# Three attentions over 4096 keys: three float32r products in place of one float32 product, in a loop over pairs of tiles

## The reference

```python
ctx_1024                     # (2, 4096, 256), keys and values alike
q = _layernorm(x) @ Wq + bq  # (2, 256, 256)
k = ctx @ Wk + bk
v = ctx @ Wv + bv
s = q @ k.T * scale          # (2, 256, 4096); layer 0 with a mask on keys
x = x + softmax(s) @ v       # layer 0: then @ Wo + bo
```

## Time and the profile before

| | us |
|---|---|
| median of 3 runs | 1531.21 (1530.9 to 1531.96) |
| profiled execution, its span | 1523.9 |
| what lies around the span, against the median | 7.3 |
| TensorE busy | 1475.2 (97%) |
| VectorE busy | 839.1 (55%) |
| ScalarE busy | 649.0 (43%) |
| GpSimd busy | 151.5 (10%) |

### The profile page before, as it was taken

The page is one execution under the profiler, slowest core; times in us unless marked ns, Lnnn a source line. Parts: engine busy times, 40 slices in busy tenths (PEclk is TensorE's granted clock), DMA queues, the critical chain, the costliest instruction groups (busy, mean ns, idle before and its releaser), DMA issues.

```text
span 1523.9 us, 24409 instructions
## 1 busy us (share of the span) xinstructions
PE 1475.2 (97%) x9937; PEld 945.5 (62%) x9937; DVE 839.1 (55%) x1502; ACT 649.0 (43%) x1231; POOL 151.5 (10%) x191
## 2 busy tenths in 40 slices
PE   8999999999999999999999999999999999999998
PEld 3668666887567755567755545555555554555697
DVE  4652645453433353333254268889999992566533
ACT  1312342212333233434263246777777777325232
POOL 0000330002100040400102050110000000100000
PEclk9999999999999999999999999999999999999999
DMA  9134132221012520103212456654675611410140
GB/s 375 64 111 172 62 110 90 89 94 50 25 55 77 209 81 8 60 28 116 97 29 106 146 126 143 95 82 67 125 166 112 125 23 72 190 56 1 53 169 14
DMA packets 42997, 147.61 MB, mean 97 GB/s; under 512 B 6380, under 2 KB 21996, under 8 KB 34028
## 3 DMA queue, kind: packets, MB, share of 16 engines
q1 hardware_dynamic: 42888, 146.07, 33.5%
HBM read 123.49 MB, written 22.56 MB: 96 GB/s over the span
## 4 chain that ended last, share of the span: by engine, by line
PE 87%; DVE 8%; ACT 3%; issue 1%; DMA 0%; SPq 0%; ACTq 0%; DVEq 0%
PE PS L162 55%; PE PS L2190 8%; PE PS L2102 7%; PE PS L2087 5%; PE PS L612 3%; PE PS L1451 2%; DVE SM L2206 2%; PE PS L1680 1%; PE PS L1701 1%; PE PS L2181 1%; PE PS L2776 1%; PE PS L1708 1%; PE PS L2681 1%; DVE SM L297 0%; DVE AR L895 0%
## 5 line engine op out<-in xcount | busy, mean ns | idle before, releaser
L2206 DVE TENSOR_REDUCE SM<-PS 128x1 f32<-128x1024 f32 x256 | 301.7, 1219 | 34.2 <-PE PS L2087 33.0
L162 PE MATMUL PS<-CT,HT 128*128 128x512 f32 x416 | 190.4, 593 | 0.7 <-ACT HT L719 0.7
L162 PE MATMUL PS<-CN,AR 128*128 128x256 f32 (+1 forms) x832 | 188.0, 371 | 0.0
L162 PEld LDWEIGHTS PS<-CN,AR 128*128 128x128 f32 x832 | 151.0, 190 | 44.0 <-issue 28.7
L2102 PE MATMUL PS<-AR 49*128 49x256 bf16 (+1 forms) x1216 | 162.8, 271 | 3.3 <-issue 2.0
L162 PE MATMUL PS<-HT,AR 128*128 128x512 f32 x328 | 150.3, 605 | 2.6 <-ACT HT L346 1.6
L2102 PE MATMUL PS<-AR,CT 49*128 49x256 bf16 (+1 forms) x832 | 124.3, 271 | 0.0
L669 DVE TENSOR_REDUCE SM<-AR 128x1 f32<-128x512 f32 x96 | 65.7, 686 | 97.2 <-ACT AR L725 95.6
L162 PEld LDWEIGHTS PS<-CT,HT 128*128 128x128 f32 x416 | 73.6, 190 | 68.4 <-issue 66.0
L162 PE MATMUL PS<-AR 128*128 128x256 f32 (+3 forms) x504 | 109.8, 372 | 1.4 <-DVE AR L647 0.8
L162 PEld LDWEIGHTS PS<-HT,AR 128*128 128x128 f32 x328 | 60.4, 192 | 76.0 <-issue 72.5
(11 more groups left out here) (373 smaller groups left out, 2118.9 us busy)
## 6 DMA issues: line engine op xcount, KB each, us to landing
CN<-ctx_n SPq DMA_DIRECT2D x24, 1024.0 KB, 4.7
AR<-k_parts SPq DMA_DIRECT2D x114, 128.0 KB
k_parts<-CN SPq DMA_DIRECT2D x32, 384.0 KB, 3.3
CT<-pack SPq DMA_DIRECT2D x6, 2048.0 KB, 8.3
AR<-pack SPq DMA_DIRECT2D x20, 512.0 KB, 4.6
CT<-k_parts SPq DMA_DIRECT2D x78, 128.0 KB
CT<-ctx_t SPq DMA_DIRECT2D x8, 1024.0 KB, 18.7
v_ones<-CN SPq DMA_DIRECT2D x28, 288.0 KB, 3.3
```

What stands on the lines that cost most here:

```text
L162: last = te.matmul(o, l, r, start=first and k == 0, stop=final and k == n - 1, skip_group_check=True)
L2206: ve.tensor_reduce(MX9[:, p % 2, e, g % 8 // 4, g % 4:g % 4 + 1], PS[:, b:b + 2, :].rearrange("p a b -> p (a b)"), AX, ALU.max).then_inc(* ...
```

## The change

`xattn` is rewritten; the rest of the program stays, but for places in AR, three waits of weight loads and the order of two things on GpSimd.

- Each operand of scores and mixes is held as a head, a copy of type float32r, and a rest, the difference between the float32 value and the head. A product becomes three: head x head, head x rest, rest x head.
- The loop runs over 16 steps g. A step is one tile and 1024 keys: `tile_of(g)`, `part_of(g)`; steps g and g + 1 (a pair of tiles) use the same two chunks of context, so a chunk k (16 in all) is split once for two tiles.
- Softmax runs over parts: VectorE takes the maximum of 1024 keys from PSUM (masked: from P), ScalarE makes the exponentials with the running maximum, and `add_mixed` rescales OB by `al`, the exponential of the change of the maximum, and adds the part.
- ScalarE makes the heads: `split_t(k)` of transposed context (128 x 1024), `split_n(k)` of context rows (128 x 1024), `head_of_weights` (128 x 512, twice a step).
- VectorE makes the rest of the weights, twice a step, and of the transposed context for k = 0 and 1; GpSimd makes it for k > 1, and the rest of the context rows for all k, in place over CN.
- Rings: context heads and rests of the transposed context 3 deep, heads of rows 3, turned weights 3, P 2, score banks 2 pairs, two banks for transposes (four from step 14), two for mixes.
- The loads of the next stages' weights wait for ("s_ps", s, 15, 1) instead of ("pt_ps", s, 2, 7); in stage 0 the mask's work tiles lie in CN, and `values_ones` runs behind the stage's GpSimd part.

In the diff below, the three loops over g are TensorE's, VectorE's and ScalarE's, in this order.

```diff
+                def score(g, h):
+                    k, t = chunk_of(g, h), tok(tile_of(g))
+                    if h == 0:
+                        _, before = SC.take(("s", s, g), ("s", s, g, 1) if masked else ("e", s, g))
+                        pe.wait_ge(*before, ("qnr", s, 0), ("qnr", s, 1))
+                    pe.wait_ge(("ctr", s, k))
+                    ch, cr = CTH[k % 3], CTR[k % 3]
+                    mm(te, PS[:, banks.of("s", s, g)[0] + h, :],
+                       [p for kt in range(2) for p in ((QNH[:, kt, t], ch[:, kt, :]), (QNH[:, kt, t], cr[:, kt, :]),
+                                                       (QNR[:, kt, t], ch[:, kt, :]))]).then_inc(
+                        *pe.inc("score", "s_ps", s, g, h))
...
+                def mix(g, h):
...
+                    pe.wait_ge(("ptr", s, g, h), ("cnr", s, k))
+                    ph, pr, nh, nr = PTH[u % 3], PTR[u % 3], CNH[k % 3], context_n(k, CNr)
+                    mm(te, bank("mix", s, g)[:, 0:256],
+                       [p for y in range(4) for p in ((ph[:, tok(y)], nh[:, y, :]), (ph[:, tok(y)], nr[:, y, :]),
+                                                      (pr[:, tok(y)], nh[:, y, :]))], h == 0, h == 1).then_inc(
+                        *pe.inc("mixed", "mix", s, g, h))
+                for g in range(2):
+                    score(g, 0)
+                    score(g, 1)
+                for g in range(14):
+                    turn(g, 0)
+                    score(g + 2, 0)
+                    turn(g, 1)
+                    mix(g, 0)
+                    score(g + 2, 1)
+                    mix(g, 1)
...
+            def rest_of_context(pr, k):
+                pr.wait_ge(("cth", s, k))
+                pr.e.tensor_tensor(CTR[k % 3], context_t(k), CTHf[k % 3], ALU.subtract).then_inc(
+                    *pr.inc("rest", "ctr", s, k))
...
+                for g in range(16):
+                    if g:
+                        add_mixed(g - 1)
+                    sums(g)
+                    rest_of_weights(g, 0)
+                    if masked and g + 2 < 16:
+                        masked_scores(g + 2, 0)
+                    rest_of_weights(g, 1)
...
+                    if g + 2 < 16:
                         if masked:
+                            masked_scores(g + 2, 1)
+                        largest(g + 2)
...
+                for g in range(16):
+                    head_of_weights(g, 0)
+                    if g + 1 < 16:
+                        exp(g + 1)
+                    head_of_weights(g, 1)
+                    if g + 4 < 16:
+                        split_t(g + 4)
+                    if g + 2 < 16:
+                        split_n(g + 2)
...
                 if s:
                     jobs_pool(pl, f"b{s}", *ht_all(s))
+                split_t(2)
+                split_n(0)
+                split_t(3)
+                split_n(1)
+                if s:
                     jobs_pool(pl, f"t{s}")
                 add_row_pool(pl, s, W["bo" if project else "bv"], *h_all(s), w, ("nb", s, 0))
+                for k in range(2, 16):
+                    if k + 2 < 16:
+                        split_t(k + 2)
+                    split_n(k)
...
-            sp.wait_ge(("pt_ps", 3, 2, 7))
+            sp.wait_ge(("s_ps", 3, 15, 1))
...
         def gpsimd_program(pl):
+            xattn_0[3](pl)
+            pl.wait_ge(("s", 0, 15, 1))
             values_ones(pl, (0, 1))
-            xattn_0[3](pl)
```

More of the change, by code:

```diff
@@ L14 @@
 I32 = mybir.dt.int32
+F32R = mybir.dt.float32r
 AX = mybir.AxisListType.X
@@ L599, in pe_part @@
                     half_pe(pe, f"h{s}", 1)
[L600 to L618, removed]
@@ L650, in dve_part @@
                 ve.tensor_copy(cadd, bank("c", s)[:, 0:4]).then_inc(*dv.inc("proj", "cadd", s))
-                for what, i, c in xattn_steps():
-                    if what == "chunk":
-                        o = S[i % 2][:, c * 512:c * 512 + 512]
-                        if masked:
[L655 to L688, removed]
@@ new lines, in dve_part, with bound @@
+                if not masked:
+                    rest_of_context(dv, 1)
+                for m in range(2):
+                    dv.wait_ge(("qnh", s, m))
+                    ve.tensor_tensor(QNR[:, m, :], bank("q2", s, m), QNHf[:, m, :], ALU.subtract).then_inc(
+                        *dv.inc("proj", "qnr", s, m))
+                if masked:
+                    rest_of_context(dv, 0)
+                    rest_of_context(dv, 1)
+                def bound(g, h):
+                    k = chunk_of(g, h)
+                    c = slice(k % 8 * 512, k % 8 * 512 + 512)
+                    dv.wait_ge(("mu", g // 8), ("s", s, *last_use(k - 8)) if k > 7 else None)
+                    ve.tensor_scalar(MB[:, c], MU[g // 8][:, c], 2 * BIG, -BIG, ALU.mult, ALU.add).then_inc(
+                        *dv.inc("bound", "bound", k))
@@ new lines, in masked_scores @@
+                def masked_scores(g, h):
+                    k = chunk_of(g, h)
+                    if g % 2 == 0:
+                        bound(g, h)
+                    dv.wait_ge(("s_ps", s, g, h), ("cadd", s), ("bound", k), ("pt_ps", s, g - 2, h) if g > 1 else None)
+                    ve.scalar_tensor_tensor(out=P[g % 2][:, h * 512:h * 512 + 512], in0=PS[:, banks.of("s", s, g)[0] + h, :],
+                                            scalar=of(cadd, tile_of(g)), in1=MB[:, k % 8 * 512:k % 8 * 512 + 512],
+                                            op0=ALU.add, op1=ALU.min).then_inc(*dv.inc("score", "s", s, g, h))
@@ new lines, in rest_of_weights @@
+                def rest_of_weights(g, h):
+                    u = 2 * g + h
+                    dv.wait_ge(("pth", s, g, h))
+                    ve.tensor_tensor(PTR[u % 3], bank("pt", s, g, h), PTHf[u % 3], ALU.subtract).then_inc(
+                        *dv.inc("turn", "ptr", s, g, h))
+                for g in range(2):
+                    if masked:
+                        masked_scores(g, 0)
+                        masked_scores(g, 1)
+                    largest(g)
+                if not ctr_by_pool(3):
+                    rest_of_context(dv, 3)
@@ L689, in dve_part @@
+                add_mixed(15)
                 if s == 0:
```

233 lines of the change are left out of this document (166 added, 67 removed).

## The result

The changed kernel takes 1560.32 us (median of 4 runs, 1556.19 to 1561.81) where the kernel before takes 1531.06 (1530.31 to 1531.96). The ratio is 1.0183, interval 1.0163 to 1.0202: **slower, by 29 us**. The forecast was 1491, its range ended at 1521. The prediction was wrong in sign, and the time lies outside its range.

What follows compares the result with a forecast made beforehand. TensorE was taken to bound the three loops; savings of 7.6, 17.0 and 15.2 us, together 39.8, cut the profiled span from 1523.9 to 1484.1, and 7.3 from span to median gave 1491 us, range 1462 to 1521.

Steps and rivals of the forecast that it cites:

- VectorE's chain: From a step's second score group to the next: 6.2 us, masked 6.98; with tile closings, steps of 6.31 and 7.09.
- three dependent small instructions at 0.18 to 0.20, 0.55: VectorE's small instructions after the reduction over 1024 scores, costed at 0.55 us of each step's chain.
- in the loops nearly all of VectorE's read PSUM: Reason given for expecting little contention between GpSimd and VectorE instructions with two SBUF inputs.
- GpSimd's late start: GpSimd's queue delays its first remainders, so TensorE waits early in each loop: 0.9, 4.35 and 6.2 us (loops 0, 3, 6).
- GpSimd paces it: Rival: GpSimd's remainders cost more, 3.08 or 3.5 us each, giving 1497 or 1519 us; chance 0.15.
- TensorE paced the kernel before: TensorE, busy nearly throughout the three loops, paces these 375 us; time falls only if it has less to do.
- One stream a float32r product, weight loads hidden: TensorE products at 0.216 us (scores) and 0.111 (mixes), making its step 6.15 us against 7.77.
- ScalarE's and GpSimd's durations: Work per step: ScalarE 4.9 us, heads of context 1.14 each; GpSimd 4.7, two remainders of 2.35; both beside TensorE's 6.15.
- Costed at nothing: Later loads of W1, W4, W7, SP's queue, values_ones and query heads add no time; uncovered, each load up to 13 us.
- two streams: Rival: a float32r product streams twice on TensorE, a step takes 11.2 us, the kernel 1705; chance 0.07.
- weight loads don't hide: Rival: each float32r load holds TensorE its whole 0.19 us, a step takes 8.04, the kernel 1559; chance 0.05.
- TensorE paces all: Rival: handoffs cheaper than counted, masked steps 6.15 instead of 7.09, no GpSimd stalls, 1462 us; chance 0.08.

Runs made afterwards that it cites:

- orders of 7: (5) with VectorE's first remainder of weights ahead of add_mixed and sums, and GpSimd's t job and additions to X later; also called experiment 7; 1490.28 us, ratio 0.9747.
- experiment 9: Changed kernel with only the two orders of 7 (remainder of weights first, GpSimd's t job and additions later), its own VectorE instructions kept; 1536.26 us, ratio 1.0041.
- experiment 1: Changed kernel with the second input of VectorE's small one-element instructions given as a pointer scalar instead of a second SBUF tensor; 1517.18 us, ratio 0.9921.
- (5): experiment 1 with the masks' bounds moved from VectorE to ScalarE; 1513.66 us, ratio 0.9879.
- experiment 6: experiment 1 with one instruction, nb (the negative of the largest), put back as a tensor_tensor of two SBUF columns; 1533.9 us, ratio 1.003.
- experiment 2: Changed kernel with each of GpSimd's context remainders as four instructions of 256 columns instead of one of 1024; 1550.78 us, ratio 1.0131.
- experiment 4: Changed kernel with only the head by head product in scores and mixes, the rests still made; single run, 1530.89 us.

## Why the prediction was wrong

The experiments make a table (us, number of the experiment; the kernel before was at 1529.5 to 1531.0 beside each):

```
                                 orders as changed    orders of 7
small ones with two SBUF inputs  1560.3               1536.3 (9)
pointer scalars                  1517.2 (1)
pointer scalars, bounds ScalarE  1513.7 (5)           1490.3 (7)
```

The pointer scalars are worth 43 us with the first orders and 1536.3 − 1490.3 − 3.5 = 42.5 with the others; the orders 24.0 and 23.4. The two causes add up, as far as a measurement tells; the 3.5 for the bounds is taken from the left column, and pointer scalars with the new orders and the bounds on VectorE were not run.

**The step that failed** is the term of VectorE's chain "three dependent small instructions at 0.18 to 0.20, 0.55", and with it the sentence that dismissed contention since "in the loops nearly all of VectorE's read PSUM". Nearly all of VectorE's *time* reads PSUM; of its *instructions* four or five a step have two SBUF inputs, and three stand one behind the other on the chain. Each can cost what GpSimd's instruction has left, not its own 0.16 us. GpSimd is busy 4.4 to 4.7 us of a step, 0.7 of the 6.3 us forecast and 0.6 of the 7.9 measured; that is the chance, estimated, that a small one which comes at any time meets it. The rows behind the term come from a stretch in which GpSimd stood still. Experiments 1, 6 and 9 show the cause: the form of the instructions alone makes 43 us, one of them 17, and the orders leave the waits in place. Two things ride on the waits: the 1.2 GHz level came with TensorE's longest waits, and GpSimd's late start weighs more. The forecast had put the clock at full speed throughout and gave neither a price. The rival "GpSimd paces it" looked at the wrong side of the same contention: it asked whether GpSimd's remainders become longer (they took 2.28) and not who waits for them.

The Trainium skill (SBUF — State Buffer, Who interferes with whom) has the rule: VectorE's second input and GpSimd share a port pair, whoever starts first has it for its whole instruction, and one SBUF input outside the two-port modes doesn't contend. The trace agrees, with ends 16 to 18 ns behind GpSimd's, and with the pointer form at 0.20 to 0.27 us under a running remainder. It differs in one point: the waits of 5.28 us (experiment 2) and 3.36 (experiment 6) went on over several of GpSimd's instructions. By the Trainium skill's rule the forecast's own rows would have given 4.7 of 6.3 us in flight and half of 2.35 left, an estimated 0.9 us for the first small instruction of a step alone.

**Step by step.**
- TensorE paced the kernel before and no longer does: right that it had to be relieved. The relief is real, 6.48 us of TensorE a step for 7.77.
- One stream a float32r product, weight loads hidden: right. Its size was off: 0.232 and 0.118 us for 0.216 and 0.111, so scores 1.38 to 1.40 for 1.30, mixes 1.41 for 1.33 and a step 6.48 for 6.15. Where TensorE paces, that is 0.17 us over the 6.31 forecast for an unmasked step, some 5 us over 28 of them.
- ScalarE's and GpSimd's durations: right (1.05 for 1.14, 2.28 to 2.40 for 2.35, additions 2.80 for 2.9 in four).
- VectorE's chain without the waits: not contradicted, and in the unmasked loops not measured, since there TensorE's 6.48 lies above the 6.31. In experiment 1 the loops' steps take 7.18, 6.89 and 7.00 us on average. The forecast, with its stalls, comes to (14 × 7.09 + 0.9) / 14 = 7.15, (14 × 6.31 + 4.35) / 14 = 6.62 and 6.75. But ten of loop 3's fourteen steps there take 6.47 to 6.53, which is TensorE's own time.
- GpSimd's late start: the mechanism and its place were right (steps 0 and 2), the size right only without the waits: in experiment 1 step 0 is 7.4 and 9.7 us and step 2 is 9.6 and 8.4, together 4.0 and 5.1 over 6.5 each, for 4.35 and 6.2 forecast. With the waits step 2 is 13.3 and 14.5. In the stretch shown, TensorE waits at step 2 for VectorE's three small ones, each behind a remainder in the unbroken run that the late start leaves to catch up; the two causes compound there, and the clock comes on top.
- In the first stage TensorE's first transposes come 2.9 us later than forecast (34.67 for 31.8). The masks' bounds are on the way: the first two took 2.61 and 1.69 us behind GpSimd's first remainders, 0.42 undisturbed. With the bounds off VectorE and the same first scores at 25.02 (experiment 7) the transposes come at 33.05, so 1.6 us are theirs. The other 1.3 fall in a stretch with a granted clock of 0.72 to 0.94 that the forecast took at full clock; that the clock makes them was not shown.
- Costed at nothing: the late loads of W1, W4 and W7 and the queue of SP cost nothing that the trace shows; from the end of loop 0 to the first scores of loop 3 it is 235.0 us in experiments 1, 7 and 9 and in the changed kernel alike (234.0 before, and 0.7 of the difference was forecast).
- Rivals: "two streams" and "weight loads don't hide" are refuted by the 415 and 287 ns records that follow one another every 0.232 and 0.118 us. "Weight loads don't hide" named 1559, which is the measured time, by a cause that isn't there. "TensorE paces all" became true in experiment 7, with the bound at 6.48 a step.

From the forecast's 313.3 us (first transposes to last mix, three loops) to the measured 371.5 it is 58.2. Of that 39.0 are the waits (to 332.5 in experiment 1), with what they cost in clock. The 19.2 left hold the dearer streams, the bounds' waits, the late start and 6.8 us at 1.2 GHz; experiments 5 and 7 bring the loops to 330.5 and 308.1.

**What stays open.** After loop 6 the changed kernel's profile has 790.3 us to the end where the profile before has 782.0, and the nine experiments have 787 to 795. Nothing in that part is changed. The traces show one difference: in that part TensorE ran at 1.2 GHz for 10.2 us in the changed kernel and for 6.8 to 13.7 in the experiments, and never in the profile before. Time at half the clock can cost at most half its length, 3.4 to 6.8 us of the 5 to 13, so the rest is open, and so is why the clock fell there. The profiled execution of before (span 1523.9, granted clock 0.998) lies at the low end of its kernel's runs, whose spans reach from 1521 to 1534: of the 43 beside the experiments, the eight with a granted clock of 0.998 and more took 1521 to 1528, the four at 0.993 and less 1533.5 to 1534.1. Why the waits last over several back-to-back GpSimd instructions in some cases (5.28 and 3.36 us) and end at the first in others isn't settled either. The order on VectorE and the order on GpSimd were not tried apart, so how the 24 us divide between them is open.

## What to carry to other kernels

When long elementwise work moves to GpSimd, look at every VectorE instruction on the path that reads two SBUF tensors, however small: it can take what GpSimd's instruction in flight has left. A one-element second input goes in as a pointer scalar, or one of the inputs is left in PSUM (those that read one input there did not wait here). Count such instructions by number and place in the chain, not by busy time. Cutting GpSimd's work into pieces helped little here (10 and 17 of the 43 us). What helps beside it is to put in front the instruction that the pacing engine waits for. And where TensorE is made to wait for long, look at the granted clock behind the wait before pricing its matmuls.

## What the runs showed of the hardware that was not expected

- A VectorE instruction of 128x1 with two SBUF inputs took up to 2.37 us beside GpSimd instructions of 2.0 to 2.4 in the changed kernel (0.15 to 0.22 alone), 3.36 over two of them back to back (experiment 6), and 5.28 beside eight back-to-back ones of 0.7; with a wait between these, 0.74 at most.
- A tensor_scalar from uint8 to bf16 with a single SBUF input waits too: 0.416 us alone, up to 2.65 beside GpSimd (experiment 9). So does one of 128x256 float32, SBUF to SBUF: 0.353 alone, 0.77 in experiment 1. Where a bound was under way when GpSimd's remainder began, the remainder took 2.55 to 2.65 us, 2.40 in the median.
- float32r at a granted clock of 1.00: 0.232 us a product of 512 columns, 0.118 for 256, in the changed kernel and in experiment 7 alike; at 0.50, 0.43 and 0.21. A 128x128 weight load of 193 to 196 ns hides behind 0.118.
- The granted clock was 0.69 to 0.77 in the loops of experiment 4, where VectorE held TensorE up in every step, and 0.96 to 1.00 in those of the changed kernel: taking work from TensorE can cost it its clock. So, by the trace, can one long wait: after 4.7 us without a matmul the clock was 0.50, and 30 of them took 6.36 us for 4.22.
